# A fused adaLN block: idle matmuls between small ones, the first transfers and the modulation columns in another order

## The reference, cut to what matters

```python
mod = silu(c) @ wmod                       # 1 x 6*256 -> sa, ca, ga, sb, cb, gb
h = layernorm(x) * (1 + ca) + sa
# attention: compress 256 -> 64 -> 32, layer norm of 32, q, k, v of 32, rope,
# causal softmax over 1024 keys, back to 64 and 256
x = x + floor(ga) * attention(h)
h = layernorm(x) * (1 + cb) + sb
# gate, up: 256 -> 2048, down: 2048 -> 256, weights in packed 4-bit codes with scales
x = x + floor(gb) * ((gelu(h @ gate) * (h @ up)) @ down)
```

## Time and profile before

| what | value |
|---|---|
| median of three runs | 225.36 us (224.93 to 226.13) |
| the profiled execution's own time | 226.4 us |
| its span, first to last instruction | 224.6 us |
| mean granted TensorE clock | 0.894 of full |
| TensorE busy | 201.5 us, 90% of the span |
| VectorE busy | 132.0 us, 59% |
| ScalarE busy | 82.6 us, 37% |

### The profile page before, as it was taken

One profiled execution on the slowest core, in us unless ns is written; L12 is line 12 of the kernel. 1 busy time (PEld: TensorE's weight loads), 2 busy tenths in 40 slices (PEclk: granted clock), 3 DMA queues, 4 the chain that ended last, 5 costly groups with the idle time before them and its releaser, 6 DMA issues.

```text
span 224.6 us, 2840 instructions
## 1 busy us (share of the span) xinstructions
PE 201.5 (90%) x1037; PEld 164.2 (73%) x1038; DVE 132.0 (59%) x246; ACT 82.6 (37%) x138; POOL 21.2 (9%) x27
## 2 busy tenths in 40 slices
PE   7899998896499559999999995989999999999991
PEld 2497568753387448888888883868788888888891
DVE  0655346757967859898898785246733233233234
ACT  2014155244687171633525433552232332232220
POOL 1412404150105100000000001000000000000000
PEclk9965578559679959999999999799999999999999
DMA  6999765300000000000000000000110000000002
GB/s 181 332 318 236 219 216 175 112 0 0 4 0 0 0 0 0 3 0 0 4 0 0 0 3 0 0 0 0 47 50 0 1 3 0 0 0 3 0 0 93
DMA packets 5645, 11.25 MB, mean 50 GB/s; under 512 B 544, under 2 KB 2752, under 8 KB 5632
## 3 DMA queue, kind: packets, MB, share of 16 engines
q1 hardware_dynamic: 5216, 10.75, 15.7%
q10 hardware_dynamic: 416, 0.33, 0.6%
HBM read 10.03 MB, written 1.05 MB: 49 GB/s over the span
## 4 chain that ended last, share of the span: by engine, by line
PE 50%; issue 31%; DVE 7%; ACT 4%; DMA 3%; POOL 3%; POOLq 0%; ACTq 0%; DVEq 0%
PE ps L846 45%; DMA a<-attn 3%; POOL WL L247 2%; PE ps L988 2%; PE ps L954 1%; DVE nmax L626 1%; DVE wmod_sb L715 1%; ACT xnT L417 1%; PE ps L871 1%; DVE xres L649 1%; ACT WH L428 1%; DVE wmod_sb L705 1%; DVE stats L555 1%; PE ps L945 1%; ACT IS L440 1%
## 5 line engine op out<-in xcount | busy, mean ns | idle before, releaser
L846 PE MATMUL ps<-H,WH 128*128 128x512 f32 x256 | 76.8, 402 | 6.3 <-ACT wmod_sb L434 5.4
L846 PEld LDWEIGHTS ps<-H,WH 128*128 128x128 f32 x256 | 46.8, 192 | 15.9 <-issue 5.5
L440 ACT ACTIVATE IS<-wmod_sb 128x512 fp32r<-128x512 f32 x32 | 20.2, 632 | 75.2 <-DVE wmod_sb L705 38.9
L846 PE MATMUL ps<-WH,IS 128*128 128x256 f32 x256 | 46.4, 284 | 0.2 <-DVE wmod_sb L715 0.2
L846 PEld LDWEIGHTS ps<-WH,IS 128*128 128x128 f32 x256 | 39.4, 191 | 2.8 <-issue 0.6
L846 PE MATMUL ps<-H,WL 128*128 128x512 f32 x128 | 40.6, 399 | 0.0
L705 DVE TENSOR_TENSOR wmod_sb<-ps,wmod_sb 128x512 f32<-128x512 f32 x32 | 22.1, 690 | 30.5 <-PE ps L846 19.5
L293 DVE TENSOR_TENSOR IS<-wmod_sb,IS 128x512 fp32r<-128x512 f32 x32 | 22.1, 691 | 28.3 <-ACT IS L440 25.6
L846 PEld LDWEIGHTS ps<-H,WL 128*128 128x128 f32 x128 | 24.5, 191 | 5.9
L846 PE MATMUL ps<-WL,IS 128*128 128x256 f32 x128 | 25.9, 283 | 0.0
L434 ACT ACTIVATE wmod_sb<-ps 128x512 f32<-128x512 f32 x32 | 18.8, 589 | 12.3 <-PE ps L846 12.3
(11 more groups left out here) (110 smaller groups left out, 202.2 us busy)
## 6 DMA issues: line engine op xcount, KB each, us to landing
W<-packed SPq DMA_DIRECT2D x8, 384.0 KB
W<-scales SPq DMA_DIRECT2D x8, 384.0 KB
xres<-x SPq DMA_DIRECT2D x2, 512.0 KB, 6.3
wmod_sb<-wmod SPq DMA_DIRECT2D x1, 1024.0 KB, 10.3
out<-xres SPq DMA_DIRECT2D x4, 256.0 KB, 2.4
wmod_sb<-wmod SPq DMA_DIRECT2D x1, 512.0 KB, 7.2
rope_sb<-rope SPq DMA_DIRECT2D x1, 512.0 KB, 10.8
cst<-consts SPq DMA_DIRECT2D x1, 258.0 KB, 5.2
```

What stands on the lines that cost most here:

```text
L440: act.activation(IS[:, b, 0, :], inter[:, b, :], ACT.Copy).then_inc(i_hi, 1)
L846: return pe.matmul(o, lhsT, rhs, start=start, stop=stop)
```

## The change

It does five things.

1. TensorE's program gets more idle matmuls: 57 in place of 20. They stand between the modulation columns, ahead of `project_c` and `transpose_c`, between the turns and the products of the attention, and behind each block of scores of the second half.
2. In TensorE's program `transpose1(0)` and the `wsum` matmul come behind the modulation columns SA and CA, and no longer ahead of them.
3. The first half of `x` is fetched in two transfers, one from SP and one from ACT. The constants are split: the identity goes from ACT with a semaphore of its own, the rest from SP behind three others. On ACT's queue both stand ahead of the transfer of `a64`.
4. VectorE does the row means of the weights (`wc_mean`, `wcc`) ahead of `norm1(0)`, and its copy of `xnT` behind the modulation columns.
5. GpSimd takes the power ahead of `wsum`.

```diff
@@ sync, scalar: the first transfers
-            sp.dma_start(xres[:, 0:HT, :], x_d[:, 0:HT, :]).then_inc(x_in[0], 16)
-            sp.dma_start(cst[:], consts).then_inc(cst_in, 16)
+            sp.dma_start(xres[:, 0:HT // 2, :], x_d[:, 0:HT // 2, :]).then_inc(x_in[0], 16)
             sp.dma_start(wmod_sb[:, :, 0:2 * D], wmod_d[:, :, 0:2 * D]).then_inc(wmod_in[0], 16)
             sp.dma_start(xres[:, HT:, :], x_d[:, HT:, :]).then_inc(x_in[1], 16)
+            sp.dma_start(cst[:, P:], consts[:, P:]).then_inc(cst_in, 16)
...
+            act.dma_start(xres[:, HT // 2:HT, :], x_d[:, HT // 2:HT, :]).then_inc(x_in0b, 16)
             act.dma_start(c_sb[:], c_col).then_inc(c_in, 16)
+            act.dma_start(cst[:, 0:P], consts[:, 0:P]).then_inc(id_in, 16)
             act.dma_start(a64[:], attn64).then_inc(a64_in, 16)
@@ gpsimd
+            rsqrt(N_LN1)
             pool.wait_ge(a64_in, 16)
             pool.tensor_tensor(wsum[:], a64[:, A_KV:A_KV + D], a64[:, A_OUT:A_OUT + D], ALU.add).then_inc(wsum_ready, 1)
-            rsqrt(N_LN1)
@@ vector
-            norm1(0)
             dve.wait_ge(wc_done, 1)
...
             link(dve.tensor_tensor(wcc[:], wc_ps, wc_mean[:].unsqueeze(2).to_broadcast([P, KT, DC]), ALU.subtract))
-            dve.wait_ge(t1_done, 1)
-            dve.tensor_copy(xnT[:, 1, :], bank(1)).then_inc(t1_ready, 1)
+            norm1(0)
...
                                   ALU.mult).then_inc(wcm_ready, 1)
+            dve.wait_ge(t1_done, 1)
+            dve.tensor_copy(xnT[:, 1, :], bank(1)).then_inc(t1_ready, 1)
@@ tensor
             last.then_inc(wc_done, 1)
-            pe.wait_ge(wsum_ready, 1)
-            mm(bank(ACC)[:, WO_C:WO_C + D], a64[:, A_LAT:A_LAT + 4 * DC], wsum[:]).then_inc(wo_done, 1)
-            stay_warm(0, 3)
-            transpose1(0)
+            stay_warm(0, 2)
             pe.wait_ge(silu_ready, 1)
             pe.wait_ge(wmod_in[0], 16)
             mod_columns(bank(MODA_B)[:, M_SA:M_SA + KT], SA, False)
+            stay_warm(0, 2)
             mod_columns(bank(MODA_B)[:, M_CA:M_CA + KT], CA, False).then_inc(moda_done, 1)
+            stay_warm(0, 1)
+            transpose1(0)
+            pe.wait_ge(wsum_ready, 1)
+            mm(bank(ACC)[:, WO_C:WO_C + D], a64[:, A_LAT:A_LAT + 4 * DC], wsum[:]).then_inc(wo_done, 1)
...
+            stay_warm(3, 2)
             project_c(0)
...
-            stay_warm(3, 1)
+            stay_warm(3, 4)
             transpose_c(0)
-            stay_warm(0, 2)
+            stay_warm(0, 3)
             project_qkv(0)
...
             transpose1(1)
+            stay_warm(0, 1)
...
-            for j in range(1, HT):
-                turn(0, j)
+            turn(0, 1)
+            stay_warm(5, 1)
+            turn(0, 2)
+            stay_warm(5, 2)
+            turn(0, 3)
             pe.wait_ge(modb_ready, 2)
-            for j in range(HT):
+            for j in range(HT - 1):
                 attend(0, j)
+            stay_warm(5, 2)
+            attend(0, HT - 1)
+            stay_warm(5, 2)
             transpose_c(1)
+            stay_warm(5, 3)
             output(0)
             project_qkv(1)
+            stay_warm(6, 2)
             stack_qk(1)
...
                 scores(1, j)
+                stay_warm(2, 3 if j else 5)
             turn(1, 0)
             turn(1, 1)
+            stay_warm(2, 2)
             transpose2(0)
```

More of the change, by code:

```diff
@@ L158, in build_block @@
         ident = cst[:, C_ID:C_ID + P]
-        x_in = [sem("x_in0"), sem("x_in1")]
+        x_in, x_in0b = [sem("x_in0"), sem("x_in1")], sem("x_in0b")
         c_in, a64_in, a32_in, cst_in, bout_in, rope_in = sem("c_in"), sem("a64_in"), sem("a32_in"), sem("cst_in"), sem("bout_in"), sem("rope_in")
+        id_in = sem("id_in")
         wmod_in = [sem("wmod_in0"), sem("wmod_in1")]
@@ L521, in add_bias @@
                 last.then_inc(xres_ready, 1)
+            rsqrt(N_LN1)
             pool.wait_ge(a64_in, 16)
             pool.tensor_tensor(wsum[:], a64[:, A_KV:A_KV + D], a64[:, A_OUT:A_OUT + D], ALU.add).then_inc(wsum_ready, 1)
-            rsqrt(N_LN1)
+            pool.wait_ge(id_in, 16)
+            pool.tensor_copy(identb[:], ident).then_inc(bf_ready, 1)
             pool.wait_ge(cst_in, 16)
-            pool.tensor_copy(identb[:], ident).then_inc(bf_ready, 1)
             pool.tensor_copy(maskb[:], cst[:, C_MASK:C_MASK + P]).then_inc(bf_ready, 1)
@@ L554, in layer_stats @@
                 for i in tiles:
+                    if k == N_LN1 and i == HT // 2:
+                        dve.wait_ge(x_in0b, 16)
                     dve.bn_stats(stats[:, i, :], xres[:, i, :]).then_inc(chain, 1)
@@ L614, in split_qk @@
             def split_qk(h):
+                dve.wait_ge(cst_in, 16)
                 dst = (QS[0:QK, h, :], KS[0:QK, HALF * h:HALF * (h + 1)])
@@ L863, in transpose1 @@
             def transpose1(h):
-                pe.wait_ge(cst_in, 16)
+                pe.wait_ge(id_in, 16)
                 if h == 1:
@@ L921, in stack_qk @@
                 pe.wait_ge(prod_ready, h + 1)
+                pe.wait_ge(cst_in, 16)
                 if h == 1:
```

## The result

The changed kernel took 231.43 us in the median of four executions (229.91 to 238.96), the kernel before 225.52 us. The ratio is 1.0239, with a 95% interval of 1.0161 to 1.0318: slower by 2.4%, where I had forecast 218.2 us and a range of 214.8 to 226.3. The profiled execution took 229.91 us against 226.4 us. Both kernels move by several microseconds from one execution to the next, with the mean granted clock; medians and ranges here have all executions, a ratio leaves out those more than 1.5% above the fastest of their kernel.

What follows compares the result with a forecast made beforehand. The prediction took the first 50 us to be mostly a chain of small matmuls at half clock. Terms of -5.7, -1.6, +0.3 and -0.2 made -7.2 us, 219.2 us profiled and 218.2 us for the median, range 214.8 to 226.3.

Steps and rivals of the forecast that it cites:

- likeliest case: Full clock up to the second half's q, k, v: 218.2 us, own range 215.5 to 220.5; chance 0.52.
- the clock falls early: Rival: clock falls before the transposes of `x` are through, as TensorE waits for `a64`; 227 to 231 us; chance 0.18.
- First transfers: Start of the kernel: `a64` comes +1.0 us later, behind half of `x`'s tiles, the identity and two more ACT issues.
- TensorE to `project_c`: From `a64` at 8.5 us, all at full clock: 6.0 us of work, so `project_c` begins at 14.5, not 13.95.
- The sum for a full clock: First scores 5.7 us earlier, near 26.3; with later terms -7.2 us, from 226.4 to 219.2 for the profiled execution.
- `attend` through `OS`: First half of the attention: products of `attend(0)` fall from 4.3 to 2.1 us; VectorE's `OS` lets -1.6 us through.
- The second `stack_qk`: Second half: clock expected to fall again in TensorE's wait for `prod`; 0 in the likeliest case, -1.7 us at best.
- The five idle matmuls between the second half's first scores: Between first and second scores: 1.1 us of idle matmuls under a row maximum of about 0.8 us, +0.3 us.
- The split of `x`: First transfers of `x` over two queues: same bytes by the same engines, costed at nothing, no time back.
- full clock throughout: Rival: the second `stack_qk` at full clock too, 216.4 us; chance 0.15, within the 0.52.
- hidden anyway: Rival: VectorE and ScalarE bound the first 32 us, so the 5.7 us shrink to nothing; 225.4 us; chance 0.08.
- The order of VectorE and GpSimd: First stage: VectorE's new order costs nothing extra, under TensorE's columns; GpSimd's power comes earlier, which nobody waits for.

Runs made afterwards that it cites:

- bridge: Changed kernel with 26 idle matmuls at the start in place of 14, late weights kept: 224.47 us, ratio 0.9852 to the kernel before.
- dense_late_a64: Changed kernel, its own transfers kept, with four idle matmuls in place of two at both places round the columns of SA: 232.83 us, ratio 1.0317.
- dense_bridge: dense_late_a64 with 26 idle matmuls at the start in place of 14: 223.34 us in the median of seven, ratio 0.9883.
- old_transfers: Changed kernel with the transfers of the kernel before, all else as changed: 223.24 us in the median of four, ratio 0.9703.
- dense_start: Changed kernel with the transfers of before and four idle matmuls in place of two at both places round the columns of SA: 219.5 us, ratio 0.9697.
- start_only: Changed kernel with the transfers of before and without the added idle matmuls from `project_c` on: 228.25 us in the median of twelve, ratio 0.995.
- only_transfers: Kernel before with the new transfers alone, no idle matmul added, no engine's order changed: 232.04 us, the kernel before 226.78 us.
- a64_first: Changed kernel with `a64` second on ACT's queue, ahead of the second quarter of `x` and the identity: 229.56 us, ratio 1.0126.

## Why the prediction was wrong

The reading of what bounds the kernel was right: small matmuls at half clock on the chain up to 50 us. The forecast put its likeliest case on the clock holding. What came is the rival "the clock falls early", for which I gave 0.18: 227 to 231 us, about 229. The 231.43 us lie just above its range. At the scores I forecast -5.7 us and the trace has +4.3. Two steps of the forecast failed.

**The first step that failed** is *First transfers*: "I take +1.0 us" for `a64`, with 1.4 us as the upper bound. It measured 2.1 us. I had worked out the bytes ahead of it, 1.4 us at most, and then let the two more issues of ACT go into the same 1.0. They add to the bytes, since `a64` starts 1.07 us later than in the earlier trace rows and then still takes 0.99 us longer. By the same bytes an upper bound of 1.07 + 1.4 = 2.5 us would have been right. By the Trainium skill ("DMA: Bandwidth & Descriptors", Issuing engines are not separate DMA queues) all transfers run on the same 16 engines and interleave; the trace agrees, the two halves of `x`, one from each queue, landed 3.2 and 3.6 us after issue. This step alone accounts for 1.1 of the 10 us between forecast and trace at the scores.

**The second step, and by far the larger,** is *TensorE to `project_c`*: "at full clock" for everything from 8.5 us on. The trace has 0.50 from 10.2 to 30.6 us. I named the condition (whether the clock is still 1.00 at the transposes) but weighed it wrongly. The wait of 2.4 us that the first step left ahead of the columns is what let it fall: filled with idle matmuls it holds to 17.5 us and the ratio goes from 1.0239 to 0.9852 (bridge), and from 1.0317 to 0.9883 (dense_late_a64 to dense_bridge). More idle matmuls behind the wait do not hold it (dense_late_a64). Whether a wait of the 1.5 us that I had forecast would have let it fall too, no run tells. Even without a wait the five idle matmuls round the columns did not always hold it: in one execution of old_transfers it fell at 10.5 us, where with nine (dense_start) it held to 28.7 behind a wait of 1.25 us.

**What stood.** The rival's working comes near the trace, in part by luck: GA at 23.0 (measured 23.23), where the start was 1.0 us too early and the rest 0.8 us too long (13.1 from the first idle matmul behind `a`, not 13.9). Further `csq` +7.0 (+7.1), and 3.6 us returned in q, k, v and `stack_qk` (3.4 from `chT,a` to the transposes behind `stack_qk`). That return hung on a clock that came back at 30.6 us; in the trace of the second run of the same kernel it came back at 40.1, and in dense_late_a64 at 38.9. The sum for a full clock stood too, though in another kernel: `stack_qk` at 22.5 and scores at 26.3 (dense_start 21.89 and 25.65), and 7.2 us for all (226.4 to 219.58, 6.8 us). There the weights came 1.2 us earlier than I had them, and four more idle matmuls cost about 0.9 us. `attend` through `OS` was given 1.6 us; from the scores to `OS` the changed kernel gained 1.6 (+4.27 to +2.63). The second `stack_qk` at half clock, as I took it, was right for the changed kernel (3.2 us).

**What else was off.** The five idle matmuls between the second half's first scores were given +0.3 us. VectorE waits 0.67 us for the second block, and its row maxima go from +2.46 to +3.22 us against before, so they cost 0.8. The split of `x` was taken at nothing; it brought the tiles 1.1 us sooner, to no use. Two sums of the rivals are off as well: by the forecast's own terms "full clock throughout" is 216.5 us, not 216.4, and "hidden anyway" is 223.9 us, not 225.4, since -1.6, +0.3 and -0.2 remain there. And the stretch ahead of 37.1 us that I called half idle had TensorE busy for 2.9 of its 3.7 us.

The order of VectorE and GpSimd I cost at nothing. start_only gives no sign against that, but its interval is 2.4% wide, so it stays unproved.

## What to carry to other kernels

One late transfer can undo idle matmuls that stand behind it: with the same nine round the columns, this kernel took 232.83 us with the wait for `a64` left open and 223.34 with it filled. When transfers are put ahead of another on a queue, add the time of each issue to the time of the bytes, and ask what TensorE does meanwhile. Fill waits by where they are, then look at the spread over executions and not at one trace: old_transfers and dense_start have the same ratio, and ranges of 10.9 and 3.5 us.

## What the runs showed of the hardware

The same kernel ran at 218.7 and at 229.6 us (old_transfers), with mean clocks of 0.961 and 0.905. The fourteen idle matmuls of the start took 4.54 us (only_transfers) to 6.10 us (old_transfers) with the same program of TensorE up to there. My estimate for one of them was 0.43 us at half clock and 0.22 at full, so I read this as a first rise to 2.4 GHz that came at another moment each time; the clock column has no record there. A higher mean clock does not say a faster kernel: the changed one had 0.918 and lost to 0.894. Two transfers more ahead of `a64` on ACT's queue delayed its issue by 1.07 us and lengthened it from 6.26 to 7.25 us; a 256 KB part of `x` took 3.6 us at the head of that queue and 8.4 us behind `a64` (a64_first).
